# Second attention: the values of four groups projected in one product, kept in memory, with new orders of the work in a unit

## What is computed

```python
q = (x @ wq).reshape(B, T, H, HD).transpose(0, 2, 1, 3)    # H = 32 heads, HD = 128
k = (x @ wk).reshape(B, T, KV, HD).transpose(0, 2, 1, 3)   # KV = 8 groups of 4 heads
v = (x @ wv).reshape(B, T, KV, HD).transpose(0, 2, 1, 3)
q = q * cos + _rotate_half(q) * sin
k = k * cos + _rotate_half(k) * sin
scores = jnp.einsum('bhtd,bhsd->bhts', q, k) * (1.0 / np.sqrt(HD))   # k, v repeated for 4 heads
att = jax.nn.softmax(jnp.where(mask, scores, -jnp.inf), axis=-1)
out = jnp.einsum('bhts,bhsd->bhtd', att, v)
return out.transpose(0, 2, 1, 3).reshape(B, T, H * HD) @ wo
```

## Time and profile before

| | us |
|---|---|
| three runs | 1361.83, 1359.53, 1360.29 |
| median | 1360.29 |
| span of the profiled execution, first to last instruction | 1357.2 |
| second attention in it, from the first matmul at 415.4 to the end of its last at about 1182 | 767 |
| one unit in the middle of it, `turn_v` to `turn_v` (677.02 to 723.74) | 46.72 |

### The profile page before, as it was taken

The page is one execution under the profiler, slowest core; times in us unless marked ns, Lnnn a source line. Parts: engine busy times, 40 slices in busy tenths (PEclk is TensorE's granted clock), DMA queues, the critical chain, the costliest instruction groups (busy, mean ns, idle before and its releaser), DMA issues. The chain is left out here.

```text
span 1357.2 us, 20247 instructions
## 1 busy us (share of the span) xinstructions
PE 1320.4 (97%) x6683; PEld 1055.9 (78%) x6683; DVE 1036.8 (76%) x2438; ACT 721.1 (53%) x1558; POOL 712.1 (52%) x641
## 2 busy tenths in 40 slices
PE   8899999998999999999999999999999999899999
PEld 6666667755776788888888888888888888688877
DVE  8888888876678887787787778777877878775553
ACT  3488887784454544454445545444544455443433
POOL 5589997773646443542444344335424433256643
PEclk9999999999999999999999999999999999999999
DMA  4000000101102110110111101101101001112222
GB/s 147 1 1 1 2 1 2 32 17 55 40 1 78 32 39 9 39 40 17 32 32 31 33 16 32 40 8 35 45 17 32 24 3 46 29 45 59 66 69 84
DMA packets 53335, 45.08 MB, mean 33 GB/s; under 512 B 4400, under 2 KB 42672, under 8 KB 52976
## 3 DMA queue, kind: packets, MB, share of 16 engines
q1 hardware_dynamic: 53232, 43.79, 10.9%
HBM read 41.69 MB, written 2.10 MB: 32 GB/s over the span
## 5 line engine op out<-in xcount | busy, mean ns | idle before, releaser
L1973 POOL TENSOR_TENSOR a_p_lo<-a_prob,a_p_hi 128x512 fp32r<-128x512 f32 x160 | 202.9, 1293 | 21.4 <-ACT a_p_hi L1817 20.7
L244 DVE CUSTOM_DVE_ANT_0 a_score<-a_score,mask_w 128x384 f32<-128x384 f32 (+3 forms) x384 | 196.6, 558 | 9.7 <-PE a_score L1396 7.0
L738 ACT ACTIVATE a_pt_hi<-a_ring 128x512 fp32r<-128x512 f32 x160 | 93.9, 597 | 161.8 <-PE a_ring L422 161.8
L896 POOL TENSOR_TENSOR a_rot_a<-a_rot_a,a_rot_b 128x512 f32<-128x512 f32 x79 | 102.3, 1295 | 146.5 <-DVE a_rot_b L600 146.5
L729 ACT ACTIVATE a_prob<-a_score,a_nmax 128x128 f32<-128x128 f32 (+3 forms) x256 | 132.0, 529 | 57.9 <-DVE a_nmax L244 57.8
L365 PE MATMUL a_xo<-h_hi,w_both 128*128 128x512 f32 x384 | 150.5, 392 | 1.8 <-DVE a_rot_b L600 1.4
L367 PE MATMUL a_xo<-h_hi,w_both 128*128 128x512 f32 x384 | 150.2, 391 | 0.0
L366 PE MATMUL a_xo<-h_lo,w_both 128*128 128x512 f32 x384 | 149.5, 389 | 0.0
L901 POOL TENSOR_TENSOR a_p_lo<-a_rot_a,a_p_hi 128x512 fp32r<-128x512 f32 x79 | 102.3, 1296 | 65.7 <-ACT a_p_hi L755 65.7
L580 DVE TENSOR_TENSOR a_pt_lo<-a_ring,a_pt_hi 128x512 fp32r<-128x512 f32 x160 | 108.6, 687 | 32.1 <-ACT a_pt_hi L738 31.1
L574 DVE TENSOR_SCALAR a_prob<-a_prob,a_rinv 128x128 f32<-128x128 f32 (+3 forms) x256 | 107.8, 464 | 4.8
(11 more groups left out here) (424 smaller groups left out, 3655.0 us busy)
## 6 DMA issues: line engine op xcount, KB each, us to landing
raw<-in_L_attn_wq SPq DMA_DIRECT2D x32, 256.0 KB, 2.9
raw<-in_L_attn_wo SPq DMA_DIRECT2D x32, 256.0 KB, 2.6
raw<-in_L_gate_up_t SPq DMA_DIRECT2D x20, 256.0 KB, 3.1
raw<-in_L_down_t SPq DMA_DIRECT2D x20, 256.0 KB, 3.0
raw<-in_L_attn_wk SPq DMA_DIRECT2D x8, 256.0 KB, 2.9
raw<-in_L_attn_wv SPq DMA_DIRECT2D x8, 256.0 KB, 2.9
out<-x SPq DMA_DIRECT2D x8, 256.0 KB, 2.5
x<-in_L_attn_x SPq DMA_DIRECT2D x3, 512.0 KB, 8.6
```

Source lines behind the costliest of these rows:

```text
L244: return nc.vector.tensor_tensor_reduce(scores, scores, m.mask_w[:, T - n:T], -1.0, LARGE, ALU.add, ALU.min, to)
L896: nc.gpsimd.tensor_tensor(of_a, of_a, of_b, ALU.add).then_inc(summed, 1)
L1973: nc.gpsimd.tensor_tensor(p_lo[:, mm % NP, :], prob[:, mm % NE, :], p_hi[:, mm % NP, :].bitcast(F32), ALU.subtract).then_inc(p_ready, 1)
```

## The change

The values are no longer projected in the units. Their weights are taken in eight pieces (128 features by 512 columns, so four groups at once), and 16 jobs `project_values(j)` multiply a tile of 128 tokens (stationary) by them, 12 matmuls of 512 columns each: 2 quads of groups, 2 sequences, 4 tiles. The result has the tokens on the partitions, so that it needs no transposes. ScalarE and VectorE split it in `ring` (`values_high`, `values_low`) into `wo_hi`, `wo_lo`, whose four slots SP writes to memory (`put_values`, 2 transfers of 256 KB a job); each unit loads its 128 columns from there straight into `p_hi`, `p_lo` (`load_values`, 2 transfers of 256 KB). Twelve jobs stand ahead of the first projection, interleaved with the layer norm of the second sequence; the last four lie between the steps of the first unit's start. `turn_v`, `read_v`, `v_high`, `v_low` and `keep_busy` fall away in this stage. The steps of a unit stand in a new order on all four engines, and the banks `xo` rotate over 9 uses instead of 11. The diff, cut to its core, with the indentation halved:

```diff
-  if k > HPG + 1:
-    h = HPG * g + k - HPG - 2
+V_PIECES, GROUP_PIECES = 8, 9
+def load_attention_piece(sp, m, inp, n):
+  slot = n % NRAW_A
+  if n < V_PIECES:
+    quad, k = divmod(n, KT)
+    src = inp["L1_attn_wv"][k * P:(k + 1) * P, quad * D:(quad + 1) * D]
+    sp.dma_start(m.raw[:, slot, :], src).then_inc(m.loaded[slot], 16)
+    return
+  g, k = divmod(n - V_PIECES, GROUP_PIECES)
+  if k > HPG:
...
   NPT = 4
-  XO_FIRST, XO_ALL = 8, 11
-  X_AT, OUT_AT, TURN_V = [-1, 0, 1, 2, 5, 6], [3, 4, 7, 9], 8
+  XO_FIRST, XO_ALL = 6, 9
+  X_AT, OUT_AT = [-1, 0, 1, 2, 5], [3, 4, 6, 7]
   OUT_LAST, LN_LAST = [-1, 0, 3, 6], [1, 2, 4, 5]
...
+        load_attention_piece(sp, m, inp, n)
+      def put_values(j):
+        quad, b, t = job(j)
+        sp.wait_ge(v_split, j + 1)
+        for e, part in enumerate((wo_hi, wo_lo)):
+          sp.dma_start(m.values[e, b, quad, t, :, :], part[:, t, :].bitcast(F32)).then_inc(v_put[t], 16)
+      def load_values(u):
+        g, b = u // 2, u % 2
+        quad, of = g // KT, g % KT
+        stored = B * quad + b + 1
+        for k in range(QT):
+          sp.wait_ge(v_put[k], 32 * stored)
+        if u >= 2:
+          sp.wait_ge(pt_used, J_ALL * (u - 1))
+        for e, part in enumerate((p_hi, p_lo)):
+          src = m.values[e, b, quad, :, :, of * P:(of + 1) * P].rearrange("t p n -> p t n")
+          sp.dma_start(part[:, b, V, :].bitcast(F32).rearrange("p (t n) -> p t n", t=QT), src).then_inc(v_loaded[b], 16)
...
+      load(weight_at(0, QT))
+      for j in range(QT, 2 * QT):
+        put_values(j)
+      load_values(0)
+      load_values(1)
+      for j in range(2 * QT, 3 * QT):
+        put_values(j)
+        load(weight_at(0, XC + j - 2 * QT))
+      for j in range(3 * QT, JOBS):
+        put_values(j)
+      for g in range(1, NG):
...
           if c >= 2:
             pe.wait_ge(rotated, c - 1)
+        elif u == 1 and c <= 1:
+          pe.wait_ge(rotated, 4 + c)
         elif c == 0:
-          pe.wait_ge(v_ready, u)
+          pe.wait_ge(added, QT * (u - 2) + 3)
         elif c == 1:
-          if u >= 2:
-            pe.wait_ge(added, QT * (u - 1))
+          pe.wait_ge(added, QT * (u - 1))
...
-        pe.wait_ge(rotated, 5 * (u + 1))
-        bank = turn_v_bank(u)
-        for t in range(QT):
-          last = nc.tensor.transpose(bank[:, t * P:(t + 1) * P], raw_v[:, t * P:(t + 1) * P], m.ident[:, :])
-        last.then_inc(v_turned, 1)
+      def project_values(j):
+        quad, b, t = job(j)
+        if b == 1 and quad == 0:
+          ln.wait(pe, t + 1)
+        if j >= 2:
+          pe.wait_ge(v_split, j - 1)
+        tok = slice((QT * b + t) * P, (QT * b + t + 1) * P)
+        for k in range(KT):
+          if j % NT == 0:
+            pe.wait_ge(w_ready, KT * quad + k + 1)
+          last = three(ring[j % 2][:, :], m.h_hi[:, k, tok], m.h_lo[:, k, tok], wv_hi[quad][:, k, :],
+                wv_lo[quad][:, k, :], k == 0, k == KT - 1)
+        last.then_inc(v_made, 1)
...
           if i == 0:
-            pe.wait_ge(v_ready, u + 1)
+            pe.wait_ge(v_loaded[b], 32 * (u // 2 + 1))
...
             pe.wait_ge(rotated, 5 * (u + 1) + i + 3)
-          elif i == 1:
-            pe.wait_ge(added, QT * u)
+          else:
+            pe.wait_ge(added, QT * u + i - 1)
         elif i == 2:
-          pe.wait_ge(rotated, 5 * (u + 2)) if u < LAST else next_ln.wait(pe, 1)
+          pe.wait_ge(added, QT * u + 2) if u < LAST else next_ln.wait(pe, 1)
         elif u < LAST:
-          pe.wait_ge(added, QT * u + 3)
+          pe.wait_ge(rotated, 5 * (u + 2))
         else:
...
+      project_values(0)
+      project_values(1)
+      project_values(2)
+      ln.turn(pe, 0)
+      ln.turn(pe, 1)
+      project_values(3)
+      ln.turn(pe, 2)
+      ln.turn(pe, 3)
+      for j in range(QT, 3 * QT):
+        project_values(j)
...
         if now:
+          weigh(u, 0, 0)
           turn(u, 1, 1)
-          scores(u, 3, 1)
-          weigh(u, 0, 0)
-          scores(u, 3, 2)
         if more:
           project(u + 1, 1)
         if now:
+          scores(u, 3, 1)
+          scores(u, 3, 2)
           turn(u, 2, 0)
           weigh(u, 1, 0)
         if more:
           project(u + 1, 2)
         if now:
-          turn(u, 2, 1)
           weigh(u, 1, 1)
         if more:
           project(u + 1, 3)
-        if u < 0 and done:
-          ln.turn(pe, 0)
         if now:
-          turn(u, 2, 2)
+          turn(u, 2, 1)
           out_project(u, 0)
           scores(u, 3, 3)
-          weigh(u, 2, 0)
-          weigh(u, 2, 1)
+          turn(u, 2, 2)
           out_project(u, 1)
           if tail:
             pe.wait_ge(added, QT * u + 1)
             next_ln.turn(pe, 0)
         if more:
...
         if now:
+          weigh(u, 2, 0)
+          weigh(u, 2, 1)
           turn(u, 3, 0)
           weigh(u, 2, 2)
+        if u < 0:
+          project_values(JOBS - 4)
+        if now:
           if tail:
             pe.wait_ge(added, QT * u + 2)
             next_ln.turn(pe, 1)
-        if more:
-          project(u + 1, V)
-        if u < 0 and done:
-          keep_busy(nc, m.ident_b, cbank, 7)
-          ln.turn(pe, 2)
-          ln.turn(pe, 3)
-          keep_busy(nc, m.ident_b, cbank, 7)
-        if now:
           turn(u, 3, 1)
           turn(u, 3, 2)
           out_project(u, 2)
+        if u < 0:
+          project_values(JOBS - 3)
+        if now:
           turn(u, 3, 3)
+        if more:
+          scores(u + 1, 0, 0)
+          scores(u + 1, 1, 0)
+          scores(u + 1, 1, 1)
+        if u < 0:
+          project_values(JOBS - 2)
+        if now:
...
-        if u < 0:
-          ln.wait(pe, ln.count)
-        if more:
-          scores(u + 1, 0, 0)
-          scores(u + 1, 1, 0)
-          scores(u + 1, 1, 1)
-        if now:
-          weigh(u, 3, 0)
-          weigh(u, 3, 1)
           weigh(u, 3, 2)
           weigh(u, 3, 3)
         if more:
           scores(u + 1, 2, 0)
-          turn_v(u + 1)
+        if u < 0:
+          project_values(JOBS - 1)
+        if more:
+          scores(u + 1, 2, 1)
           turn(u + 1, 0, 0)
-          scores(u + 1, 2, 1)
           scores(u + 1, 2, 2)
         if now:
           out_project(u, 3)
         if more:
           turn(u + 1, 1, 0)
-          scores(u + 1, 2, 3)
         if then:
           project(u + 2, 0)
         if more:
+          scores(u + 1, 2, 3)
           scores(u + 1, 3, 0)
...
+      def values_low(j):
+        dve.wait_ge(v_hi_done, j + 1)
+        nc.vector.tensor_tensor(wo_lo[:, j % QT, :], ring[j % 2][:, :], wo_hi[:, j % QT, :].bitcast(F32),
+                    ALU.subtract).then_inc(v_split, 1)
...
+      ln.scales(dve)
+      ln.rows(dve, 0)
+      values_low(0)
+      ln.rows(dve, 1)
+      ln.rows(dve, 2)
+      values_low(1)
+      ln.low(dve, 0)
+      ln.rows(dve, 3)
+      values_low(2)
...
+          low(u, 2, 2)
           normalise(u, 3, 0)
...
+          normalise(u, 3, 1)
           add_out(u, 1)
+        if more:
+          rotate(u + 1, 4)
+        if now:
...
+          low(u, 3, 0)
+        if u < 0:
+          values_low(JOBS - 4)
+          values_low(JOBS - 3)
         if now:
-          low(u, 3, 0)
...
           head_low(u, 3)
+        if u < 0:
+          values_low(JOBS - 2)
         if more:
           maxima(u + 1, 2, 0)
           normalise(u + 1, 1, 1)
+        if u < 0:
+          values_low(JOBS - 1)
+        if more:
+          maxima(u + 1, 2, 1)
+          maxima(u + 1, 2, 2)
           low(u + 1, 0, 0)
-          v_low(u + 1)
-          maxima(u + 1, 2, 1)
         if now:
           add_out(u, 3)
         if more:
-          maxima(u + 1, 2, 2)
           maxima(u + 1, 2, 3)
           normalise(u + 1, 2, 0)
+          low(u + 1, 1, 0)
           normalise(u + 1, 2, 1)
-          low(u + 1, 1, 0)
...
-          low(u + 1, 2, 0)
           maxima(u + 1, 3, 0)
-          maxima(u + 1, 3, 1)
         if then:
           rotate(u + 2, 2)
         if more:
+          maxima(u + 1, 3, 1)
+          low(u + 1, 2, 0)
           head_low(u + 1, 1)
           maxima(u + 1, 3, 2)
-          low(u + 1, 2, 1)
         if then:
           rotate(u + 2, 3)
         if more:
+          low(u + 1, 2, 1)
           add_out(u + 1, 0)
           maxima(u + 1, 3, 3)
...
+      def values_high(j):
+        act.wait_ge(v_made, j + 1)
+        if j >= QT:
+          act.wait_ge(v_put[j % QT], 32 * (j // QT))
+        nc.scalar.activation(wo_hi[:, j % QT, :], ring[j % 2][:, :], ACT.Copy).then_inc(v_hi_done, 1)
...
+      values_high(0)
       ln.roots(act)
...
           head_high(u, 0)
...
+        if late:
+          weights_high(g + 1, 4)
...
           high(u, 2, 0)
+          head_high(u, 1)
...
+          exponentials(u, 3, [0])
+          high(u, 2, 1)
...
         if now:
-          high(u, 2, 1)
-          head_high(u, 1)
-          exponentials(u, 3, [0])
+          exponentials(u, 3, [1, 2])
+          high(u, 2, 2)
         if more:
           part_high(u + 1, 2)
```

(93 more changed lines are left out.)

234 lines of the change are left out of this document (118 added, 116 removed).

## The result

| | kernel before | changed kernel |
|---|---|---|
| median of 4 runs each, us | 1359.97 (1359.53 to 1361.83) | 1374.13 (1372.23 to 1375.06) |
| span of the profiled execution, us | 1357.2 | 1372.6 |

The ratio is 1.0101, with a 95% interval of 1.0086 to 1.0115: 14 us slower, where 11.5 were forecast (1371.8 in a range of 1354 to 1379).

The account below looks back on a forecast made before the run. The units were taken as bound by TensorE alone. Projection 0, turning -7.0, start -6, last unit -1 and waits 15 x 1.7 = +25.5 gave +11.5 on the median 1360.3: 1371.8 us, range 1354 to 1379.

Parts of the forecast that it names:

- The unit: From weigh(u, 0, 0) to the next: 43.5 us plus a TensorE wait of 1.7, so 45.2.
- the race: VectorE's fourth scaling against GpSimd's subtraction of product 3: GpSimd wins by 0.06 us, wait 1.7 instead of 0.78.
- the chain: weigh(u, 2, 2) over head_high, head_low to out_project(u, 2): 2.36 us against 1.58, 0.78 of waiting a unit, +11.7.
- the two turns' 0.79 + 0.79: TensorE work left between weigh(u, 2, 2) and out_project(u, 2): 1.58 us, where 4.32 stood before.
- rival 3: More scalings held up by GpSimd in the units, late transfers or a dearer start: 1377 to 1381; chance 10%.
- The count of the streams: Four engines' steps timed from weigh(u, 0, 0): first scaling 18.7 us, third 21.35, GpSimd's subtraction 21.69, out_project 27.3.
- rival 1: The fourth scaling comes ahead of GpSimd, only 0.78 of waiting a unit is left: -2.3, 1358; chance 26%.
- The name of the wait: TensorE's waits name a_c_lo at out_project, 15 entries of 1.3 to 1.6, some at turn(u, 3, 2) for a_pt_lo.
- Turning and projection: Four transposes fewer a unit, 16 x 0.44 = -7.0; jobs of 2.74 us replace the values' projections, 0 in sum.
- Start: Start of stage: idle time, keep_busy and restarts save 8.6, waits for job 2's bank and GpSimd's splits add 2.6: -6.
- Memory: Values' round trip, 32 transfers out and 32 back, asked for some 40 us ahead: 0.
- The end of the stage: The last unit's new order: -1 of its 4.8 us idle (-3 to +2).

Follow-up runs that it names:

- experiment 1: Changed kernel with GpSimd made to wait for normalise(u, 3, 1) before part_low(u + 1, 3): 1359.06 us, ratio 0.9989 to the kernel before.
- experiment 6: Changed kernel with out_project(u, 1) and project(u + 1, 4) exchanged, ScalarE's splits moved and a GpSimd wait for normalise(u, 3, 1) added: 1347.81 us, ratio 0.9914.
- experiment 2: Kernel before with weigh(u, 2, 2) moved behind project(u + 1, V), the work unchanged: 1373.24 us, ratio 1.0084.
- Experiment 3: Changed kernel with the units' steps on all four engines in the orders of the kernel before, less those that fell away: 1374.91 us, ratio 1.0101.
- experiment 8: Kernel of experiment 6 with values_low(0) moved between the two halves of the layer norm's chain on VectorE: 1346.31 us, ratio 0.9899.
- experiment 5: Changed kernel with every load of a unit's values made twice, the second after the first has landed: 1373.15 us, ratio 1.0100.
- experiment 4: Changed kernel with the four scalings of 512 columns as products of two tensors instead of products with a scalar: 1387.66 us, ratio 1.0191.

## Why the prediction was right, and where it was off

Between the same instructions of the two profiles, in us:

| stretch | forecast | measured |
|---|---|---|
| ahead of the stage | 0 | 416.68 - 415.42 = +1.3 |
| first matmul of the stage to the first `weigh(u, 0, 0)` | +33.6 | 71.42 - 38.20 = +33.2 |
| 14 units | -20.7 | 633.92 - 654.09 = -20.2 |
| from unit 14's first weigh to the last `out_project`'s end | -1.4 | 75.23 - 74.16 = +1.1 |
| behind it | 0 | 175.30 - 175.29 = 0 |
| sum | +11.5 | +15.4 |

The forecasts are the terms of the sum laid on these points. The start is 16 jobs of 2.74, less one projection and one turning of values, less 6, less the 1.04 of `scores(0, 3, 1)` and `turn(0, 1, 1)`, which now stand behind the weigh. A unit is 1.7 - 2.74 - 0.44 = -1.48. The end is the same -3.18 + 1.7, the -1, and the 1.04 again.

- **The unit: right, in mechanism and size.** Forecast 45.2, measured 45.28. Of the wait, experiment 1 gives the race 45.28 - 44.41 = 0.87 (forecast 1.7 - 0.78 = 0.92) and experiment 6 the chain 44.41 - 43.65 = 0.76 (forecast 0.78; experiment 2, in the other kernel, 0.83). What the prediction calls the two turns' 0.79 + 0.79 is the weigh's own 0.79 and 0.79 for both turns (710.13 to 710.92 and 713.66 to 714.45); the sum is the same. The further meetings of rival 3 didn't reach TensorE: in the units it waits at this one place. Experiment 3 shows the one thing the forecast didn't say: with the old order the loss would have been the same.
- **The count of the streams: right to some 0.1 us.** The first scaling of `normalise(u, 3, 0)` was put to 18.7 us behind the first weigh and came at 687.78 - 669.19 = 18.6; the third scaling to 21.35, it came at 21.4; GpSimd's third instruction to 21.69, it came at 21.7. The race, with a margin forecast at 0.06, was lost by about 0.06, and in the same way in all 14 units (1.25 idle in each). That a count by hand has its sign right at a gap as small as this is in part luck; it could have fallen the other way, and rival 1's 26% said so.
- **The name of the wait: wrong.** 15 entries for `a_c_lo` at `out_project` were to be seen, with some of the wait at `turn(u, 3, 2)`; 15 stand at `turn(u, 3, 2)` for `a_pt_lo`, with nearly all of it. VectorE takes `low(u, 3, 0)` just ahead of `head_low(u, 2)`, and the turn stands ahead of `out_project`, so the first of two late results has nearly all of the wait, and the second one some 0.2 (the matmul at 696.47 starts at the end of `a_c_lo`, 696.41). Both end with the same stream; the price is unchanged.
- **Turning and projection: right.** A unit without waits is 46.72 - 43.65 = 3.07 shorter in experiment 6, against 2.74 + 0.44 = 3.18.
- **Start: right.** The forecast was 2.6 of added waits at two places, and the waits are 1.7 for job 2's bank and 0.6 for GpSimd's last split, at these places; experiment 8 shows the first one's cause.
- **Memory: right.** 0, by experiment 5.
- **The end of the stage: mis-sized by 2.5.** The wait of unit 14 is 1.97 instead of 1.25, since `add_out(14, ...)` there takes a statistic of 0.7 as well, which the count for a middle unit didn't have; and 1.5 are a stretch at half clock right behind it (below), which belongs to this one execution: experiment 5, with the same units, doesn't have it.
- **1.3 us ahead of the stage** lie in work that is the same in both kernels and belong to the execution: with the same code ahead of it, the first matmul of the stage starts at 415.45 in experiment 5's profile, and between 415.3 and 417.5 in all ten. The runs of one kernel differ by 2 to 3 us. Between the medians, which are 14.2 apart, the sum is off by 2.7.

## What to carry to other kernels

Work on the bounding engine that is taken out may have been the cover of a chain through other engines: before counting its time as won, write down what stood between the chain's first and last step, what stands there now, and how long the chain is where it shows bare. When the bound gets shorter and the other engines' work doesn't, lay their streams side by side in microseconds. Here that gave the loss to within 0.1 us a unit, and the whole mend of 26 us needed both halves at once (a cover for the chain, and GpSimd's work kept off VectorE's SBUF-to-SBUF instructions).

## What the runs showed of the hardware

Two SBUF inputs are enough for a VectorE instruction and a GpSimd one that reads SBUF to exclude each other (experiment 4). The subtractions that read a PSUM bank are not held up: `a_c_lo` starts at 695.73, in the midst of a GpSimd sum (695.17 to 696.45), and takes its 0.68, and the sum takes its 1.28.

In the second attention of the changed kernel's profile the clock fell once. Windows around the wait of unit 14, a matmul from there, then a window of experiment 5 that begins 0.8 ahead of the end of the same wait (1.97), and one of experiment 4 behind its wait of 2.26; PEclk is the third figure from the end:

```profile
1147.00:1149.40 2.40, 0.46 (x5) 0.21 (x2) 2.34 (x5) 1.08 (x2) 0.67 (x1) 1.00 0.00 0
...
1150.20:1153.40 3.20, 3.20 (x8) 2.53 (x9) 1.06 (x2) 0.95 (x2) 1.28 (x1) 0.51 0.00 0
...
1151.04 0.63 PE L426 MATMUL a_xo<-a_wo_hi,a_c_lo 128*128 128x512 f32 x1
...
1147.60:1150.80 3.20, 2.41 (x12) 1.92 (x13) 2.55 (x5) 1.12 (x2) 2.37 (x2) 1.00 0.00 0
...
1165.00:1175.00 10.00, 10.00 (x60) 8.79 (x59) 7.83 (x32) 5.42 (x19) 1.39 (x2) 1.00 0.00 0
```

TensorE had been busy for 0.46 of 2.40 us, then ran for some 3 us at the lower level (0.51, 1.2 GHz): matmuls 0.43 apart instead of 0.23, 1.5 us lost (from the waiting turn's start to the next turn's 4.99, in experiment 5 3.49). The same wait in experiment 5, and the one of 2.26 in experiment 4, left the clock at 1.00, so the length of the wait alone doesn't decide it; what does is left open.
